# A mixture-of-experts stage on one Trainium2 core: the second layer's bias moved from a matmul into the copy out of PSUM

## The chip, the cores and the metric

The kernel runs on one core of one Trainium2 chip. The metric is the device time of one execution, in microseconds (us), lower is better. All inputs and outputs are float32 arrays in the chip's memory (HBM).

## The reference, cut to what matters

The program is one network of two layers on an input of 2 x 256 x 48 x 48. Layer 0 is a selective scan on images, layer 1 is attention and then a feed-forward block with eight experts, of which each of the 4608 tokens uses two. Only the last block is touched:

```python
logits = xf @ gate_w + gate_b
probs = softmax(logits)
top2_vals, top2_idx = top_k(probs, 2)
cw = zeros((N, 8)).at[arange(N)[:, None], top2_idx].add(top2_vals)
# for each expert, with bb1 of 512 and bb2 of 256 numbers:
h = gelu(xf @ w1 + bb1)
y = h @ w2 + bb2
acc = acc + we[:, None] * y
```

xf is 4608 x 256, w1 is 256 x 512, w2 is 512 x 256 for each expert.

## The kernel before, in words

The program is a row of phases with a barrier of all engines between them. The scan takes most of the span, then come the attention, a blend with the gate's logits, `gate_phase` (L1727) and `expert_phase` (L1956). The instructions of every engine are written out by hand in their order, with a semaphore for each hand-over. The experts' loop is unrolled.

`gate_phase` sorts the 9216 pairs of token and expert by expert and cuts the sorted list into 79 tiles (`TILES`) of 128 rows, each with one expert. It leaves `we["from"]` and `we["to"]` (the row numbers for gather and scatter), `we["own"]` (the expert of each tile, integers) and `we["sel"]`. It also splits the second layer's weights into a high part on ScalarE (L1829) and a low part on GpSimd (L1800), and makes `we["rows"]`: 40 partitions that hold the biases of the eight experts in rows 0 to 7 (high part) and 32 to 39 (low part, L1940), zero between; 512 columns of the first bias and 256 of the second.

`expert_phase` runs over the 79 tiles. For tile i:

- GpSimd gathers 128 rows of the tokens (`gather`, L1989) two tiles ahead, makes `sel` (L1994), a 40 x 128 matrix that has a one in the rows of the tile's expert, and scatters the tile's result (`scatter`, L1998).
- TensorE turns the rows (`turn_x`, L2032, two transposes), multiplies by the first layer (`up`): the bias comes first, as a matmul of `sel` with 512 columns of `rows` (L2040, 40 rows deep), then six matmuls of 512 columns (L2045 to L2047). It turns the hidden values (`turn_h`, L2055, four transposes) and multiplies by the second layer (`down`): the bias first, as a matmul of `sel` with 256 columns of `rows` (L2062, 40 rows deep), then twelve matmuls of 256 columns (L2067 to L2069). All products go as three passes of high and low parts.
- The weights are addressed with a register that `value_load` reads from `we["own"]` once per tile (before `up`).
- ScalarE makes the high part of x (L2100), the gelu (L2107) and the high part of h (L2113). VectorE makes the low parts (L2131, L2147) and copies the result out of PSUM into one of three buffers (`move_y`, L2137), which the scatter reads.

The order on TensorE is `up(i)`, `turn_x(i+1)`, `down(i-1)`, `turn_h(i)`, and on VectorE the low part of x(i+1), `move_y(i-1)`, the low part of h(i). In both, tile i-1's end lies between pieces of tile i:

```python
for i in range(TILES):
    e = pe.value_load(we["own"][0:1, i:i + 1], min_val=0, max_val=E - 1)
    up(i, e)
    if i + 1 < TILES:
        turn_x(i + 1)
    if i:
        down(i - 1, before)
    turn_h(i)
    before = e
```

After the loop SyncE waits for all scatters and loads the results back in 12 steps (L2023), VectorE joins them with their weights (L2157, L2163), TensorE turns them (L2091), ScalarE copies them (L2122) and stores. The loads go to three pairs of buffers: `yb00`, `yb01`, `yb10`, the memory of `table`, and that of `xy`.

Of the kernel before, what the change touches and what calls it, by code (L numbers as in the profile page):

```python
# [8 lines left out]
F32R = mybir.dt.float32r  # L9
U32 = mybir.dt.uint32  # L10
I32 = mybir.dt.int32
ALU = mybir.AluOpType
# [3 lines left out]
B, C, H, W = 2, 256, 48, 48  # L16
# [20 lines left out]
TT = 384  # L37
# [5 lines left out]
E, HF = 8, 512  # L43
HB = HF // 128
TILES = 2 * NT // 128 + E - 1
FAR = 8192
BROWS = 40
# [1679 lines left out]
def gate_phase(nc, P, w, keep, we, route):  # L1727
# [5 lines left out]
    with ExitStack() as ctx:  # L1733
        s = Space(nc, ctx, "gate")
        raw = [s.sb(f"raw{i}", [128, 2 * HF]) for i in range(2)]
        rows = s.sb("rows", [BROWS, HF + C])
        small = lambda name, n=E, dt=F32: s.sb(name, [128, KB, n], dt)
        dif = route["lg"]
        dif2, ex2, pick = (small(n, 2) for n in ("dif2", "ex2", "pick"))
# [11 lines left out]
        own = s.sb("own", [128, TILES])  # L1751
# [10 lines left out]
        hi_cut, lo_cut, rows_here, zeroed, rows_cut, zero_out = (s.sem(n) for n in ("hi_cut", "lo_cut", "rows_here", "zeroed", "rows_cut", "zero_out"))  # L1762
# [7 lines left out]
        @block.sync  # L1770
        def _(sp):
            def weights(n):
                if n >= 2:
                    sp.wait_ge(lo_cut, n - 1)
                sp.dma_start(raw[n % 2][:, :].rearrange("p (h n) -> p h n", h=HB), w["W2"][n].rearrange("(h p) n -> p h n", h=HB)).then_inc(raw_here[n % 2], 16)

            weights(0)
            weights(1)
            sp.wait_ge(zeroed, 1)
            sp.dma_start(P["xt"][0:1, :], rows[E:E + 1, 0:C]).then_inc(zero_out, 16)  # L1780
            for at in (0, 32):
                sp.dma_start(rows[at:at + E, 0:HF], w["b1"]).then_inc(rows_here, 16)
                sp.dma_start(rows[at:at + E, HF:HF + C], w["b2"]).then_inc(rows_here, 16)
            for n in range(2, E):
                weights(n)
            sp.wait_ge(zero_out, 16)
# [38 lines left out]
        @block.scalar  # L1825
        def _(act):
            def cut(n):
                act.wait_ge(raw_here[n % 2], 16 * (n // 2 + 1))
                act.activation(piece(n, "_hi"), raw[n % 2][:, :], ACT.Copy).then_inc(hi_cut, 1)  # L1829

            def name_low(b):
                act.wait_ge(e_done, b + 1)
                if b >= 2:
                    act.wait_ge(listed, b - 1)
                act.activation(hot_q[b % 2][:, :, 1, :], hot_e[b % 2][:, :, :], ACT.Identity, scale=row1[:, 0:1]).then_inc(l_done, 1)

            cut(0)
            cut(1)
            cut(2)
            act.wait_ge(step_done, 2)  # L1840
            act.activation(dif[:, :, :], dif[:, :, :], ACT.Exp).then_inc(ex_done, 1)
            act.activation(ex2[:, :, :], dif2[:, :, :], ACT.Exp).then_inc(ex_done, 1)
            cut(3)
            act.wait_ge(rows_here, 64)
            act.activation(we["rows"][:, :], rows[:, :], ACT.Copy).then_inc(rows_cut, 1)
            for n in range(4, E):
                cut(n)
            act.wait_ge(row_done, 2)
            for b in range(NH):
                name_low(b)  # L1850
# [102 lines left out]
            dve.tensor_tensor(we["to"][:, :], ids[:, :], spare[:, :], ALU.add)  # L1953


def expert_phase(nc, P, keep, acc, we, table, out):  # L1956


    with ExitStack() as ctx:
        s = Space(nc, ctx, "moe")  # L1960
        ring = lambda name, n, shape, dt=F32: [s.sb(f"{name}{i}", shape, dt) for i in range(n)]
        XR, YR = 3, 3
        xy = s.sb("xy", [128, XR + YR, C])
        xg, yo = [xy[:, i, :] for i in range(XR)], [xy[:, XR + i, :] for i in range(YR)]
        x_hi, x_lo = ring("x_hi", 2, [128, 2, 128], F32R), ring("x_lo", 2, [128, 2, 128], F32R)
        sel = ring("sel", 3, [BROWS, 128], F32R)
        g = ring("g", 2, [128, HF])
        h_hi, h_lo = ring("h_hi", 2, [128, HB, 128], F32R), ring("h_lo", 2, [128, HB, 128], F32R)
        TR = 3
        yb = [[s.sb(f"yb{i}{c}", [128, TT // 128, C])[:, :, :] for c in range(2 - i)] for i in range(TR - 1)] + [[xy[:, c * 3:c * 3 + 3, :] for c in range(2)]]  # L1970
        yb[1].append(table[:, 0:2 * TT].rearrange("p (a c) -> p a c", c=C))
        ps_x, ps_h, ps_t, ps_y = ([s.ps(f"{n}{i}", [128, 512]) for i in range(2)] for n in ("ps_x", "ps_h", "ps_t", "ps_y"))
        came = [s.sem(f"came{i}") for i in range(XR)]
        sent = [s.sem(f"sent{i}") for i in range(YR)]
        x_turned, xh_done, xl_done, up_done, g_done, h_turned, hh_done, hl_done, down_done, y_moved, sel_done = (
            s.sem(n) for n in ("x_turned", "xh_done", "xl_done", "up_done", "g_done", "h_turned", "hh_done", "hl_done", "down_done", "y_moved", "sel_done"))
        out_gone = s.sem("out_gone")
        y_here = [s.sem(f"y_here{i}") for i in range(TR)]
        first_done, both_done, back_done, out_done = (s.sem(n) for n in ("first_done", "both_done", "back_done", "out_done"))
        BL = TT // 128  # L1980
# [31 lines left out]

        @block.sync
        def _(sp):
            for k in range(YR):
                sp.wait_ge(sent[k], 16 * ((TILES + YR - 1 - k) // YR))

            for t in range(NTT):
                if t >= TR:
                    sp.wait_ge(back_done, t - TR + 1)  # L2020
                for c in range(2):
                    at = 1 + FAR * c + t * TT
                    sp.dma_start(yb[t % TR][c], P["y2"][at:at + TT, :].rearrange("(a p) n -> p a n", p=128)).then_inc(y_here[t % TR], 16)  # L2023

        @block.tensor
        def _(pe):
# [31 lines left out]
            def down(i, e):  # L2058
                if i >= 2:
                    pe.wait_ge(y_moved, i - 1)  # L2060
                o = ps_y[i % 2][:, 0:C]
                pe.matmul(o, sel[i % 3][:, :], we["rows"][:, HF:HF + C], start=True, stop=False)  # L2062
                pe.wait_ge(hl_done, i + 1)
                for b in range(HB):
                    w_hi = we["w2_hi"][:, bass.ds(e * (HB * C) + b * C, C)]
                    w_lo = we["w2_lo"][:, bass.ds(e * (HB * C) + b * C, C)]
                    pe.matmul(o, h_hi[i % 2][:, b, :], w_lo, start=False, stop=False)  # L2067
                    pe.matmul(o, h_lo[i % 2][:, b, :], w_hi, start=False, stop=False)  # L2068
                    mm = pe.matmul(o, h_hi[i % 2][:, b, :], w_hi, start=False, stop=b == HB - 1)  # L2069
                mm.then_inc(down_done, 1)  # L2070
# [3 lines left out]
            for i in range(TILES):  # L2074
                e = pe.value_load(we["own"][0:1, i:i + 1], min_val=0, max_val=E - 1)
# [50 lines left out]
        @block.vector  # L2126
        def _(dve):
            def cut_x(i):
                dve.wait_ge(xh_done, i + 1)
                v = lambda x: x[:, :, :].rearrange("p a b -> p (a b)")  # L2130
                dve.tensor_tensor(v(x_lo[i % 2]), ps_x[i % 2][:, 0:C], v(x_hi[i % 2]).bitcast(F32), ALU.subtract).then_inc(xl_done, 1)  # L2131

            def move_y(i):
                dve.wait_ge(down_done, i + 1)
                if i >= YR:
                    dve.wait_ge(sent[i % YR], 16 * (i // YR))
                dve.tensor_copy(yo[i % YR][:, :], ps_y[i % 2][:, 0:C]).then_inc(y_moved, 1)  # L2137

            cut_x(0)
            for i in range(TILES):  # L2140
                if i + 1 < TILES:
                    cut_x(i + 1)
                if i:
                    move_y(i - 1)
                dve.wait_ge(hh_done, i + 1)
                v = lambda x: x[:, :, :].rearrange("p a b -> p (a b)")
                dve.tensor_tensor(v(h_lo[i % 2]), ps_t[i % 2][:, :], v(h_hi[i % 2]).bitcast(F32), ALU.subtract).then_inc(hl_done, 1)  # L2147
            move_y(TILES - 1)

            half = lambda v: v.rearrange("p (h c) -> p h c", h=2)  # L2150

            def join(t):
                dve.wait_ge(y_here[t % TR], 32 * (t // TR + 1))
                for a in range(BL):
                    n = t * BL + a
                    v = half(yb[t % TR][0][:, a, :])
                    dve.scalar_tensor_tensor(v, v, we["v"][:, n, 0:1],  # L2157
                                             acc[:, :, n * 128:n * 128 + 128], ALU.mult, ALU.add).then_inc(first_done, 1)
                for a in range(BL):
                    n = t * BL + a  # L2160
                    dve.wait_ge(first_done, n + 1)
                    v = yb[t % TR][0][:, a, :]
                    dve.scalar_tensor_tensor(v, yb[t % TR][1][:, a, :], we["v"][:, n, 1:2], v, ALU.mult, ALU.add).then_inc(both_done, 1)  # L2163

            for t in range(NTT):
                join(t)


def conv_attn_hybrid_kernel(nc, x, w0, w1, out):
# [12 lines left out]
    with ExitStack() as ctx:  # L2182
# [41 lines left out]
        blend_phase(nc, P, w1, keep, t_hi, t_lo, o_t, den, we["w1_hi"], we["w1_lo"], route)  # L2224
        turns.close()
        we |= {n: s.sb(n, [128, E * HB * C], F32R) for n in ("w2_hi", "w2_lo")}
        we["rows"], we["sel"] = s.sb("rows", [BROWS, HF + C], F32R), s.sb("sel", [BROWS, TILES])
        we["v"], we["own"] = s.sb("v", [128, KB, 2]), s.sb("own", [1, TILES], I32)
        we["from"], we["to"] = s.sb("from", [128, TILES], I32), s.sb("to", [128, TILES], I32)
        gate_phase(nc, P, w1, keep, we, route)  # L2230
        expert_phase(nc, P, keep, o_t, we, table, out)


_L0 = ["ln_g", "ln_b", "skip_scale", "proj_W", "proj_b", "in_W", "conv_W", "conv_b", "x_proj_W", "dt_W", "dt_b",
# [19 lines left out]
```

## Time and profile before

| | |
|---|---|
| median of 3 runs | 5875.48 us (5871.67 to 5880.47) |
| the profiled execution's own time | 5875.91 us |
| its span in the trace | 5874.2 us |
| TensorE busy | 5065.8 us, 86% |
| GpSimd busy | 4271.6 us, 73% |
| VectorE busy | 4213.8 us, 72% |
| ScalarE busy | 3787.4 us, 64% |

PE is TensorE's matmuls, PEld its weight loads, DVE VectorE, ACT ScalarE, POOL GpSimd, SP SyncE. A matmul is shown from its start to a modelled end, and overlaps the next one, so the start-to-start distance is what it occupies. "[idle before <-x]" at a row's end says how long the engine had been idle and what ended that; "issue" means that it waited for nothing that the profile shows. The expert loop lies in the stretch from 5449 to 5822 us of the span, the loads and stores after it end the span.

### The profile page before, as it was taken

How to read it: one execution, taken by the hardware profiler on the slowest of the kernel's cores; microseconds unless marked ns; L12 is line 12 of the kernel's file. 1: busy time of each engine (PE TensorE's matmuls, PEld its weight loads, DVE VectorE, ACT ScalarE, POOL GpSimd, SP SyncE). 2: the span in 40 equal slices, each digit the busy share in tenths (PEclk: the TensorE clock that was granted, in tenths of full speed). 3: DMA queues.
4: the chain of work that ended last, by engine and by line, in shares of the span. 5: the costliest groups of instructions: out<-in, count | busy, mean ns of one | idle time of the engine just before them, and what ended most of it. 6: DMA issues, size and time to landing. Idle time of an engine off the chain costs nothing. (4 is left out here: it accounts for less than half of the span.)

```text
span 5874.2 us, 82875 instructions
## 1 busy us (share of the span) xinstructions
PE 5065.8 (86%) x21540; PEld 3376.1 (57%) x21540; DVE 4213.8 (72%) x4029; ACT 3787.4 (64%) x8376; POOL 4271.6 (73%) x2720
## 2 busy tenths in 40 slices
PE   4777388998899899889998999897799999995997
PEld 2344255555555555555555555554458888884675
DVE  3677599999999999999999999997751111118334
ACT  2566588888888888888888888885442222226332
POOL 0567699999999899999998999997504444444442
PEclk8888599999999999999999999998999999996998
DMA  3666677777777777777777777777500000004113
GB/s 94 171 198 205 209 235 247 249 246 251 240 246 248 241 247 246 244 248 243 243 249 239 248 245 247 249 248 263 194 23 1 0 0 0 0 0 123 50 58 132
DMA packets 395504, 1045.37 MB, mean 178 GB/s; under 512 B 53422, under 2 KB 90319, under 8 KB 390944
## 3 DMA queue, kind: packets, MB, share of 16 engines
q1 hardware_dynamic: 382464, 1010.05, 54.1%
q0 software_dynamic: 7584, 20.72, 1.1%
q10 hardware_dynamic: 4992, 9.44, 0.4%
q8 instruction: 166, 2.72, 0.2%
q14 instruction: 298, 2.44, 0.1%
HBM read 869.23 MB, written 170.79 MB: 177 GB/s over the span
## 5 line engine op out<-in xcount | busy, mean ns | idle before, releaser
L920 POOL TENSOR_TENSOR scan_hc<-scan_h,scan_c_rep 128x768 f32<-128x768 f32 x1536 | 2749.2, 1821 | 233.9 <-PE scan_ps_y L751 177.2
L751 PE MATMUL scan_ps_y<-scan_hc,keep_ident 128*128 128x512 f32 (+1 forms) x6144 | 2219.8, 489 | 23.4 <-ACT scan_y L786 23.0
L885 DVE TENSOR_TENSOR_SCAN scan_h<-scan_da,scan_h,scan_ps_p 128x768 f32<-128x768 f32 x896 | 1568.7, 1796 | 0.0
L751 PEld LDWEIGHTS scan_ps_y<-scan_hc,keep_ident 128*128 128x128 f32 x6144 | 1067.9, 190 | 824.1 <-issue 739.3
L803 ACT ACTIVATE scan_warm<-scan_du_t 128x128 f32<-128x128 f32 x4608 | 1423.6, 388 | 38.7 <-PE scan_ps_p L742 32.9
L842 ACT ACTIVATE scan_da<-scan_dd,layer_a_neg 128x768 f32<-128x768 f32 x1344 | 1184.8, 922 | 4.4 <-issue 3.6
L1464 POOL TENSOR_TENSOR attn_e_lo<-attn_e,attn_e_hi 128x512 fp32r<-128x512 f32 x324 | 418.1, 1290 | 610.9 <-DVE attn_e_hi L1455 610.9
L742 PE MATMUL scan_ps_p<-keep_ident,scan_warm 128*128 128x128 f32 x4608 | 647.9, 277 | 222.2 <-DVE scan_h L885 221.3
L885 DVE TENSOR_TENSOR_SCAN scan_h<-scan_da,scan_ps_p 128x768 f32<-128x768 f32 x448 | 758.9, 1735 | 2.3 <-ACT scan_da L842 2.0
L742 PEld LDWEIGHTS scan_ps_p<-keep_ident,scan_warm 128*128 128x128 f32 x4608 | 532.7, 141 | 372.2 <-issue 156.9
L864 DVE TENSOR_TENSOR scan_ps_p<-scan_ps_p,scan_dd 128x768 f32<-128x768 f32 x576 | 547.5, 951 | 194.2 <-PE scan_ps_p L734 193.0
L1455 DVE CAST attn_e_hi<-attn_e 128x512 fp32r<-128x512 f32 x324 | 145.8, 450 | 725.4 <-ACT attn_e L1443 725.4
L1443 ACT ACTIVATE attn_e<-attn_ps_s 128x512 f32<-128x512 f32 x324 | 193.8, 598 | 708.1 <-PE attn_ps_s L74 708.1
L734 PE MATMUL scan_ps_p<-scan_cut,layer_b_sel 128*128 128x512 f32 (+1 forms) x1152 | 381.8, 413 | 57.4 <-DVE scan_h L885 47.8
L842 ACT ACTIVATE scan_ps_p<-scan_dd,layer_a_neg 128x768 f32<-128x768 f32 x192 | 172.2, 897 | 274.9 <-DVE scan_h L885 274.9
L914 POOL TENSOR_TENSOR scan_bu<-scan_dd,scan_b_rep 128x768 f32<-128x768 f32 x192 | 348.2, 1814 | 0.0
L575 POOL TENSOR_TENSOR delta_de<-delta_de,delta_du 128x768 f32<-128x768 f32 x96 | 173.1, 1811 | 193.5 <-ACT delta_du L488 193.5
L734 PEld LDWEIGHTS scan_ps_p<-scan_cut,layer_b_sel 128*128 128x128 f32 x1152 | 196.4, 190 | 156.0 <-DVE scan_h L885 131.8
L74 PE MATMUL attn_ps_o<-attn_e_hi,t_hi 128*128 128x512 f32 x648 | 257.9, 398 | 0.0
L74 PE MATMUL attn_ps_s<-f_hi 128*128 x648 | 257.1, 397 | 0.0
L73 PE MATMUL attn_ps_o<-attn_e_lo,t_hi 128*128 128x512 f32 x648 | 256.8, 396 | 0.0
L72 PE MATMUL attn_ps_o<-attn_e_hi,t_lo 128*128 128x512 f32 x648 | 256.3, 396 | 0.0
(328 smaller groups left out, 6910.4 us busy)
## 6 DMA issues: line engine op xcount, KB each, us to landing
scan_c_rep<-bc_dram SPq DMA_DIRECT2D x1536, 384.0 KB, 4.2
scan_dd<-dd_dram SPq DMA_DIRECT2D x96, 768.0 KB, 5.7
scan_b_rep<-bc_dram SPq DMA_DIRECT2D x192, 384.0 KB, 4.9
dd_dram<-delta_de SPq DMA_DIRECT2D x96, 384.0 KB, 2.6
dd_dram<-delta_du SPq DMA_DIRECT2D x96, 384.0 KB, 3.2
y_dram<-scan_y SPq DMA_DIRECT2D x96, 384.0 KB, 4.6
mid_nat<-y_dram SPq DMA_DIRECT2D x48, 384.0 KB, 7.8
delta_img<-xn_dram SPq DMA_DIRECT2D x16, 576.0 KB, 8.6
```

What stands on the lines that cost most here:

```text
L73: pe.matmul(out, wh, xl, start=False, stop=False)
L74: return pe.matmul(out, wh, xh, start=False, stop=stop)
L734: mm = pe.matmul(ps_p[place(t) % PR][:, lo:hi], keep["b_sel"][:, n, :], cut[st % 2][:, lo:hi], start=True, stop=True)
L742: mm = pe.transpose(ps_p[place(t) % PR][:, b * 128:b * 128 + 128], warm[w % WR][:, b, :], keep["ident"][:, :])
L751: mm = pe.matmul(ps_y[:, lo:hi], keep["ident"][:, :], hc[t % HR][:, lo:hi], start=n == 0, stop=n == N - 1)
L803: last = act.activation(warm[w % WR][:, b, :], du_t[st % 2][:, b * 128:b * 128 + 128], ACT.Identity, scale=du_t[st % 2][:, at:at + 1])
L842: act.activation(dst, dd[st % 2][:, 0, :], ACT.Exp, scale=keep["a_neg"][:, k, n:n + 1]).then_inc(ex_done, 1)
L864: dve.tensor_tensor(x, x, dd[st % 2][:, 1, :], ALU.mult).then_inc(mult_done, 1)
L885: dve.tensor_tensor_scan(view(h[n]), view(x), view(y), start, ALU.mult, ALU.add).then_inc(scan_done, 1)
L914: pool.tensor_tensor(bu[f % SR][:, :], dd[st % 2][:, 1, :], b_rep[f % SR][:, :], ALU.mult).then_inc(bu_done, 1)
L920: pool.tensor_tensor(hc[t % HR][:, :], h[t % N][:, :], c_rep[t % CR][:, :], ALU.mult).then_inc(hc_done, 1)
L1464: pool.tensor_tensor(e_lo[j % 3][:, :], e[j % 3][:, :], e_hi[j % 3][:, :].bitcast(F32), ALU.subtract).then_inc(lo_done, 1)
```

## The change

The 40-row table keeps the first layer's bias alone (512 columns in place of 768), and the matmul L2062 is gone. The first of the twelve matmuls of `down` now opens the accumulation. At the start of the phase SyncE issues one DMA that copies the second layer's 8 x 256 biases to every one of the 128 partitions (2048 numbers each, 1 MB written), into a new tile `desk`, which after the loop serves as three of the buffers that the results are loaded back to. VectorE waits for it once, ahead of the loop. In `move_y` VectorE now loads the tile's expert number into a register of its own and adds, in place of copying, PSUM and the 256 columns of `desk` that the register names. In `gate_phase` the two small DMAs of the second bias go, and the copy and the low part of `rows` are 512 columns wide.

```diff
-        rows = s.sb("rows", [BROWS, HF + C])
+        rows = s.sb("rows", [BROWS, HF])
...
                 sp.dma_start(rows[at:at + E, 0:HF], w["b1"]).then_inc(rows_here, 16)
-                sp.dma_start(rows[at:at + E, HF:HF + C], w["b2"]).then_inc(rows_here, 16)
...
-            act.wait_ge(rows_here, 64)
+            act.wait_ge(rows_here, 32)
...
-        yb = [[s.sb(f"yb{i}{c}", [128, TT // 128, C])[:, :, :] for c in range(2 - i)] for i in range(TR - 1)] + [[xy[:, c * 3:c * 3 + 3, :] for c in range(2)]]
-        yb[1].append(table[:, 0:2 * TT].rearrange("p (a c) -> p a c", c=C))
+        desk = s.sb("desk", [128, 3, 2 * TT])
+        add_y = desk[:, :, :].rearrange("p a c -> p (a c)")[:, 0:E * C]
+        third = lambda x: x.rearrange("p (a c) -> p a c", c=C)
+        yb = [[third(desk[:, 0, :]), third(desk[:, 1, :])], [third(desk[:, 2, :]), third(table[:, 0:2 * TT])], [xy[:, c * 3:c * 3 + 3, :] for c in range(2)]]
...
         @block.sync
         def _(sp):
+            sp.dma_start(add_y, w["b2"].rearrange("e c -> (e c)").partition_broadcast(128)).then_inc(add_here, 16)
...
                 o = ps_y[i % 2][:, 0:C]
-                pe.matmul(o, sel[i % 3][:, :], we["rows"][:, HF:HF + C], start=True, stop=False)
                 pe.wait_ge(hl_done, i + 1)
...
-                    pe.matmul(o, h_hi[i % 2][:, b, :], w_lo, start=False, stop=False)
+                    pe.matmul(o, h_hi[i % 2][:, b, :], w_lo, start=b == 0, stop=False)
...
-                dve.tensor_copy(yo[i % YR][:, :], ps_y[i % 2][:, 0:C]).then_inc(y_moved, 1)
+                e = dve.value_load(we["own"][0:1, i:i + 1], min_val=0, max_val=E - 1)
+                dve.tensor_tensor(yo[i % YR][:, :], ps_y[i % 2][:, 0:C], add_y[:, bass.ds(e * C, C)], ALU.add).then_inc(y_moved, 1)
 
             cut_x(0)
+            dve.wait_ge(add_here, 16)
```

On TensorE, between `turn_x` and the twelve matmuls of `down`, there stood before:

```order
L2047 MATMUL moe_ps_h<-w_hi,moe_x_hi 128x512
L2032 MATMUL moe_ps_x<-keep_ident,moe_xy 128x128 x2
L2062 MATMUL moe_ps_y<-keep_rows,moe_sel 128x256
L2067 REGISTER_ALU
L2067 MATMUL moe_ps_y<-keep_w_lo,moe_h_hi 128x256
L2068 REGISTER_ALU
L2068 MATMUL moe_ps_y<-keep_w_hi,moe_h_lo 128x256
L2069 MATMUL moe_ps_y<-keep_w_hi,moe_h_hi 128x256
```

and now (the lines of `down` are one further, those of `turn_x` and `up` two):

```order
L2049 MATMUL moe_ps_h<-w_hi,moe_x_hi 128x512
L2034 MATMUL moe_ps_x<-keep_ident,moe_xy 128x128 x2
L2068 REGISTER_ALU
L2068 MATMUL moe_ps_y<-keep_w_lo,moe_h_hi 128x256
L2069 REGISTER_ALU
L2069 MATMUL moe_ps_y<-keep_w_hi,moe_h_lo 128x256
L2070 MATMUL moe_ps_y<-keep_w_hi,moe_h_hi 128x256
```

One matmul per tile is gone, 79 in all, and a matmul of full depth follows the transposes directly; nothing else of TensorE's order moved.

On VectorE one tile of the loop read before (`xh_done`, `down_done` and `hh_done` are the semaphores of x's high part, of `down` and of h's high part):

```order
L2131 TENSOR_TENSOR moe_x_lo<-moe_ps_x,moe_x_hi 128x256 [waits moe_xh_done]
L2137 COPY moe_xy<-moe_ps_y 128x256 [waits moe_down_done]
L2147 TENSOR_TENSOR moe_h_lo<-moe_ps_t,moe_h_hi 128x512 [waits moe_hh_done]
L2131 TENSOR_TENSOR moe_x_lo<-moe_ps_x,moe_x_hi 128x256 [waits moe_xh_done]
L2137 COPY moe_xy<-moe_ps_y 128x256 [waits moe_down_done]
```

and now:

```order
L2132 TENSOR_TENSOR moe_x_lo<-moe_ps_x,moe_x_hi 128x256 [waits moe_xh_done]
L2138 TENSOR_LOAD keep_own [waits moe_down_done]
L2138 ISA x2
L2139 ISA
L2139 TENSOR_TENSOR moe_xy<-moe_ps_y,moe_desk 128x256
L2150 TENSOR_TENSOR moe_h_lo<-moe_ps_t,moe_h_hi 128x512 [waits moe_hh_done]
```

The register load and three register instructions stand behind the wait for `down`, ahead of the addition, and the low part of h is behind all of them.

## Rows read from the trace of the kernel before

**Rows 1.** Busy time of each engine in two stretches; clock, DMA share, GB/s at the end
```profile
5455.00:5820.00 365.00, 363.56 (x2040) 282.50 (x2038) 120.94 (x235) 116.00 (x237) 172.58 (x231) 0.99 0.17 56
5820.00:5875.00 55.00, 20.13 (x84) 15.12 (x84) 29.82 (x73) 10.47 (x24) 0.97 (x1) 0.54 0.78 262
```

**Rows 2.** Timeline, TensorE around L2062 in one tile: start us, us, instruction
```profile
5603.90 0.38 PE L2032 MATMUL moe_ps_x<-keep_ident,moe_xy 128*128 128x128 f32 x2
...
5604.21 0.18 PEld L2062 LDWEIGHTS moe_ps_y<-keep_rows,moe_sel 40*128 40x128 f32 x1 [0.17 <-issue]
5604.21 0.38 PE L2062 MATMUL moe_ps_y<-keep_rows,moe_sel 40*128 40x256 f32 x1
5604.52 0.19 PEld L2067 LDWEIGHTS moe_ps_y<-keep_w_lo,moe_h_hi 128*128 128x128 f32 x1
5604.52 0.39 PE L2067 MATMUL moe_ps_y<-keep_w_lo,moe_h_hi 128*128 x1
...
5604.62 0.19 PEld L2068 LDWEIGHTS moe_ps_y<-keep_w_hi,moe_h_lo 128*128 128x128 f32 x1
5604.74 0.28 PE L2068 MATMUL moe_ps_y<-keep_w_hi,moe_h_lo 128*128 x1
...
5604.86 0.29 PE L2069 MATMUL moe_ps_y<-keep_w_hi,moe_h_hi 128*128 x1
...
5605.95 0.47 PEld L2055 LDWEIGHTS moe_ps_t<-keep_ident,moe_g 128*128 128x128 f32 x4
5606.05 0.60 PE L2055 MATMUL moe_ps_t<-keep_ident,moe_g 128*128 128x128 f32 x4
...
5608.81 0.38 PE L2062 MATMUL moe_ps_y<-keep_rows,moe_sel 40*128 40x256 f32 x1
```

**Rows 3.** Timeline of TensorE in the scan: 16-row transposes followed by 128-row matmuls
```profile
3977.71 0.54 PE L725 MATMUL scan_ps_p<-keep_ident,scan_rows 16*128 16x16 f32 x6
3978.30 0.62 PE L734 MATMUL scan_ps_p<-scan_cut,layer_b_sel 128*128 128x512 f32 x2
...
3978.30 0.30 PEld L734 LDWEIGHTS scan_ps_p<-scan_cut,layer_b_sel 128*128 128x128 f32 x2
```

**Rows 4.** Timeline of TensorE in the scan: 128-row transposes followed by 128-row matmuls
```profile
3001.78 0.84 PE L742 MATMUL scan_ps_p<-keep_ident,scan_warm 128*128 128x128 f32 x6
3002.46 1.02 PE L751 MATMUL scan_ps_y<-scan_hc,keep_ident 128*128 128x512 f32 x2
...
3002.35 0.30 PEld L751 LDWEIGHTS scan_ps_y<-scan_hc,keep_ident 128*128 128x128 f32 x2
```

**Rows 5.** Timeline, VectorE in the same tile as rows 2
```profile
5606.25 0.42 DVE L2137 COPY moe_xy<-moe_ps_y 128x256 f32<-128x256 f32 x1 [0.82 <-PE moe_ps_y L2069]
...
5607.32 0.69 DVE L2147 TENSOR_TENSOR moe_h_lo<-moe_ps_t,moe_h_hi 128x512 fp32r<-128x512 f32 x1 [0.64 <-ACT moe_h_hi L2113]
```

**Rows 6.** Timeline, end of the gate phase and the first tiles
```profile
5446.39 0.95 DVE L1940 TENSOR_TENSOR keep_rows<-gate_rows,keep_rows 8x768 fp32r<-8x768 f32 x1
...
5449.72 1.17 POOL L1989 DMA_INDIRECT moe_xy<-xt_dram,keep_from  x1 [24.27 <-POOLq L1733]
...
5452.76 0.69 PE L2032 MATMUL moe_ps_x<-keep_ident,moe_xy 128*128 128x128 f32 x2 [6.37 <-DMA moe_xy<-xt_dram,keep_from]
...
5453.65 0.78 PE L2040 MATMUL moe_ps_h<-keep_rows,moe_sel 40*128 40x512 f32 x1 [0.21 <-issue]
...
5458.34 0.42 DVE L2131 TENSOR_TENSOR moe_x_lo<-moe_ps_x,moe_x_hi 128x256 fp32r<-128x256 f32 x1 [4.01 <-ACT moe_x_hi L2100]
```

**Rows 7.** Timeline, the last tile
```profile
5818.08 0.42 DVE L2137 COPY moe_xy<-moe_ps_y 128x256 f32<-128x256 f32 x1 [2.63 <-PE moe_ps_y L2069]
...
5818.41 0.38 PE L2062 MATMUL moe_ps_y<-keep_rows,moe_sel 40*128 40x256 f32 x1
...
5819.15 0.69 DVE L2147 TENSOR_TENSOR moe_h_lo<-moe_ps_t,moe_h_hi 128x512 fp32r<-128x512 f32 x1 [0.64 <-ACT moe_h_hi L2113]
...
5819.97 0.36 PE L2067 MATMUL moe_ps_y<-keep_w_lo,moe_h_hi 128*128 x1 [1.18 <-DVE moe_h_lo L2147]
```

More of the change, by code:

```diff
@@ L1953, in _, with expert_phase @@
             dve.tensor_tensor(we["to"][:, :], ids[:, :], spare[:, :], ALU.add)
-def expert_phase(nc, P, keep, acc, we, table, out):
+def expert_phase(nc, P, w, keep, acc, we, table, out):
     with ExitStack() as ctx:
@@ L1976, in expert_phase @@
             s.sem(n) for n in ("x_turned", "xh_done", "xl_done", "up_done", "g_done", "h_turned", "hh_done", "hl_done", "down_done", "y_moved", "sel_done"))
-        out_gone = s.sem("out_gone")
+        out_gone, add_here = s.sem("out_gone"), s.sem("add_here")
         y_here = [s.sem(f"y_here{i}") for i in range(TR)]
@@ L2226, in conv_attn_hybrid_kernel @@
         we |= {n: s.sb(n, [128, E * HB * C], F32R) for n in ("w2_hi", "w2_lo")}
-        we["rows"], we["sel"] = s.sb("rows", [BROWS, HF + C], F32R), s.sb("sel", [BROWS, TILES])
+        we["rows"], we["sel"] = s.sb("rows", [BROWS, HF], F32R), s.sb("sel", [BROWS, TILES])
         we["v"], we["own"] = s.sb("v", [128, KB, 2]), s.sb("own", [1, TILES], I32)
@@ L2230, in conv_attn_hybrid_kernel @@
         gate_phase(nc, P, w1, keep, we, route)
-        expert_phase(nc, P, keep, o_t, we, table, out)
+        expert_phase(nc, P, w1, keep, o_t, we, table, out)
 _L0 = ["ln_g", "ln_b", "skip_scale", "proj_W", "proj_b", "in_W", "conv_W", "conv_b", "x_proj_W", "dt_W", "dt_b",
```

## The prediction

> **What bounds the kernel now.** Read first the busy time by stretch, over the experts' loop [rows 1]: of 365 us TensorE is busy for 363.56, VectorE for 120.94, ScalarE for 116.00, GpSimd for 172.58, at full clock (0.99). The loop is TensorE's, and the other engines only matter by when they answer. Then the timeline of one tile [rows 2]: the bias matmul L2062 starts at 5604.21 and again at 5608.81, so a tile takes 4.60 us, and 79 tiles make the loop. The reader is to look in rows 2 at where each weight load (PEld) starts against its matmul (PE). For L2068 the load starts 0.12 us ahead of its matmul, beside the matmul before; the same for L2055. For L2062 and for L2067, the one right behind it, load and matmul start together: the load lies open. Third, VectorE's rows of that tile [rows 5], for how late its work may come, and last the two ends of the loop [rows 6, 7], for the new DMA and for what the tail waits on.
>
> **The matmul that goes.** From the start of the two transposes L2032 (5603.90) to the start of L2068 (5604.74) there are 0.84 us [rows 2]. Without L2062, and with every load hidden, the same stretch is two transposes and one matmul of 256 columns. A 128-row transpose takes 0.11 us start to start (six in 0.84 with the last one's 0.28: (0.84 - 0.28) / 5) [rows 4], a 256-column matmul 0.12 (5604.74 to 5604.86) [rows 2]: 0.34 us. So up to 0.84 - 0.34 = **0.50 us a tile** go. Of this, 0.31 are L2062's own distance to L2067 (5604.21 to 5604.52), the rest is what the switch to 40 rows and back adds to its two neighbours: L2067 occupies 0.22 in place of 0.12, and L2062 starts 0.20 in place of 0.11 after the second transpose.
>
> Does the rest go too? It depends on why L2067's load isn't hidden. Two readings: the change of depth from 40 rows to 128, or the wait and register instruction ahead of L2067, which stay. The wait is a poor cause: L2055 also stands behind waits, and its load is hidden (5605.95 against 5606.05) [rows 2]; L2068 stands behind a register instruction and is hidden too. The depth is the better one: in the scan a 128-row matmul follows 16-row transposes, and its load starts with it, at 3978.30, after the last of these has ended (3977.71 + 0.54) [rows 3]; where 128-row matmuls follow 128-row transposes the load starts at 3002.35, 0.11 ahead of its matmul and while the transposes still run [rows 4]. The changed kernel has the latter case: L2034 (128 rows), then L2068 (128 rows). I take 0.50 us. The lower bound is 0.31.
>
> Here two rules of the Trainium skill part. "TensorE: Matmul & The Clock Gate", in Part 3 on packing small matmuls, says that a weight load overlaps matmuls in flight only when its row group differs; by it a full-depth load behind full-depth transposes would stay open, and the sum would have 0.31 a tile. "TensorEngine Tiling (Array Packing)", Key Properties, says that changing the tiling mode drains the engine; by it the sum has 0.50. The trace agrees with the second and not with the first (rows 4, a load at 3002.35 beside transposes of the same depth).
>
> How often: all tiles but the last. In the last one L2062 starts at 5818.41 and L2067 at 5819.97, released by the low part of h [rows 7]: the bias matmul lies in a gap. 78 x 0.50 = **-39.0 us** (lower bound 78 x 0.31 = -24.2).
>
> **The addition in place of the copy.** The two read the same 256 columns of PSUM and write the same buffer; the nearest row for the addition is L2131 at 0.42 us [rows 6], a tensor_tensor of PSUM and SBUF of that size, and the copy takes 0.42 [rows 5]. Nothing.
>
> **The register load on VectorE.** No row shows a TENSOR_LOAD. On TensorE one stands, with two ISA instructions, between the first two transposes and the first L2040: 5452.76 to 5453.65 = 0.89 us, of which the transposes take most [rows 6]. So for the load and its companions, L, the rows give between 0 and 0.89; VectorE has three companions, not two, and can't start before `down` has ended. I take 0.8, near the upper row. Is it hidden? After the copy (ends 5606.67) VectorE waits until 5607.32, so 0.65 are free; the low part of h then ends at 5608.01, and the down matmuls that want it start at 5608.81 (0.80 later, 0.7 with the new order) [rows 2, 5]. So L up to about 1.3 costs nothing in the loop. As a cycle: from L2067's start to the copy's 1.73 us (5604.52 to 5606.25), less the 0.10 that L2067 loses, then L, 0.42 of addition, 0.69 of low part, some 0.05 of hand-overs: 2.79 + L against a tile of 4.10. The cover is the `up` of the next tile; without it L would be paid in full. It is paid at the end: the last `move_y` is alone (+0.8), and the one before it, at 5818.08, now ends at 5819.30, so that the last low part of h starts 0.2 later than 5819.15 [rows 7]. **+1.0 us**. The skill has a price for the load: "DMA: Bandwidth & Descriptors", Latency and other measured facts, gives a tensor_load a floor of about 600 ns; no run here shows it, and with 0.6 in place of 0.8 the sum would be 0.3 lower.
>
> **The scatter behind it.** GpSimd's scatter waits for `y_moved` and stands ahead of the next gather, so both move by L. GpSimd is busy 172.58 of 365 us [rows 1], and a gather is issued two tiles, over 8 us, ahead of its transposes. Nothing.
>
> **The broadcast.** SyncE writes 1.05 MB (128 x 8 KB) while the first gather is under way: the gather starts at 5449.72 and the first transposes wait for it until 5452.76, idle 6.37 us [rows 6]. At the 262 GB/s of the tail [rows 1] the broadcast takes 4.0 us. Bounds: the gather is served beside it as if alone, 0; or wholly behind it, 4.0. I take the middle, **+2.0 us**. The wait on VectorE costs nothing: it stands ahead of the x part of tile 1, at 5458.34, over 8 us after the phase's start [rows 6].
>
> **The gate phase.** The low part of `rows` (0.95 us for 768 columns) is in VectorE's chain that ends the phase [rows 6]; with 512 columns it takes 0.95 x 512/768 = 0.63: **-0.3 us**. The missing small DMAs, the narrower copy and fill lie on engines that are waiting there. Nothing.
>
> **The tail.** Same number and size of loads, to other addresses; `desk` is read last long before the loads, which wait for all scatters. Nothing.
>
> **Sum**: -39.0 + 1.0 + 2.0 - 0.3 = -36.3. The profiled execution took 5875.9, hence 5839.6; the median of the runs is 0.4 below it, hence **5839 us**.
>
> **The rivals.**
> - *The open load stays* (0.31 a tile). For it: in the trace no 128-row matmul of this reduced type behind transposes is looked at in this loop, and the wait for h's low part stays ahead of it. Against it: rows 3 and 4. -24.2 + 2.7 = -21.5: 5854 us. The first of the skill's two rules above gives the same.
> - *VectorE's chain binds in part*: L between 1.3 and 1.8. At 1.6 a tile is 4.39 and 78 x 0.21 = 16.4 are gained: about 5862 us. Against it: 0.89 is more than TensorE's load can have taken.
> - *Slower: VectorE's chain becomes the bound.* The register load begins only when `down(i-1)` has ended, the low part of h(i) stands behind it, and `down(i)` waits for that. At L = 2.0 a tile takes 4.79 us in place of 4.60: 78 x 0.19 = +14.8, with +2 for the gather and +3 at the end about 5895 us. It decides from L = 1.81. For it: nothing measures the load on VectorE. Against it: the same 0.89.
> - *No difference*: L near 1.8, or a bound in the loop that these rows don't show (a late gather, instruction supply) that holds the tile at 4.6 us. 5875 us. That the change doesn't do what it says can be set aside: the order has the 79 matmuls gone.
>
> **How the numbers follow.** Forecast 0.64; load stays open 0.22; VectorE in part 0.06; slower 0.05; no difference 0.03. About 0.2% (12 us) is what a measurement of this kernel can tell from no change; the three runs lie within 9 us. Faster by more: 0.64 + 0.22 + 0.06 = 0.92; same 0.03; slower 0.05. The forecast's own range is 5875.5 - 39.0 - 0.3, with 0 to 4.0 for the gather and 0 to 1.8 for the end: 5836 to 5842, and some 3 us more on either side for the runs' scatter. The rival at 0.31 gives with the same bounds up to 5857. Range 5833 to 5858.
>
> **What would show it.** The distance from one tile to the next 4.10 us, TensorE still busy throughout; the weight load of the first `down` matmul 0.1 us ahead of its matmul (if it starts with it, the first rival holds, with 4.3 us a tile). VectorE: the addition at 0.42 us, its idle time before it longer by L, the low part of h still released by ScalarE or by VectorE's own row before it, never TensorE waiting for it except in the last tile. The first transposes at 5452.8 + 0 to 4 us. The tail unchanged in length. The prediction is wrong in its reason if TensorE's idle time names VectorE's low part of h in every tile.

## The result, and the profile after

| | before | changed |
|---|---|---|
| median | 5875.46 us (5863.97 to 5880.47, 5 runs) | 5829.36 us (5825.08 to 5840.02, 5 runs) |
| span of the profiled execution | 5874.2 us | 5827.6 us |
| TensorE busy | 5065.8 us | 5022.8 us |

The ratio is 0.9934, with a 95% interval of 0.9922 to 0.9945: 32 to 46 us less. The forecast was 5839 us, 36 less. Cut at four points of the two traces, the spans differ like this:

| stretch | before | changed | difference |
|---|---|---|---|
| start to the first gather's issue | 5449.72 | 5440.25 | -9.47 |
| to the first transposes | 3.04 | 4.34 | +1.30 |
| to the start of the last `move_y` operation | 368.90 | 329.69 | -39.21 |
| to the end | 52.54 | 53.32 | +0.78 |

Only the middle two rows are the change's. The first is nearly all run-to-run spread of phases that the change leaves alone: over the twelve profiled executions of this study the first gather was issued between 5438.78 and 5454.61 us, whichever kernel it was, and the changed kernel and its variants spread over that whole width. The change's own part of it is the narrower low part of `rows`, 0.27 us (below).

The changed kernel's busy time by stretch, as [rows 1] (PE, PEld, DVE, ACT, POOL, then clock, DMA share, GB/s), over the loop and over what follows it:

```profile
5450.00:5774.00 324.00, 321.92 (x1964) 264.40 (x1964) 113.93 (x235) 115.19 (x235) 172.20 (x229) 1.00 0.19 63
5774.00:5827.00 53.00, 18.49 (x72) 13.69 (x72) 29.90 (x73) 10.46 (x24) 0.97 (x1) 0.53 0.80 270
```

TensorE is still busy throughout. The timeline of the changed kernel around the place where L2062 stood, as [rows 2]:

```profile
5604.20 0.38 PE L2034 MATMUL moe_ps_x<-keep_ident,moe_xy 128*128 128x128 f32 x2
5604.31 0.19 PEld L2068 LDWEIGHTS moe_ps_y<-keep_w_lo,moe_h_hi 128*128 128x128 f32 x1
5604.33 0.36 PE L2068 MATMUL moe_ps_y<-keep_w_lo,moe_h_hi 128*128 x1
...
5604.41 0.19 PEld L2069 LDWEIGHTS moe_ps_y<-keep_w_hi,moe_h_lo 128*128 128x128 f32 x1
5604.53 0.28 PE L2069 MATMUL moe_ps_y<-keep_w_hi,moe_h_lo 128*128 x1
...
5605.72 0.28 PE L2070 MATMUL moe_ps_y<-keep_w_hi,moe_h_hi 128*128 x1
...
5608.43 0.36 PE L2068 MATMUL moe_ps_y<-keep_w_lo,moe_h_hi 128*128 x1
```

From 5604.33 to 5608.43 there are 4.10 us, as forecast. From the first transposes to L2069 there are 0.33 us (0.84 before). The load is hidden: L2069 follows its two predecessors without the 0.1 or 0.2 us that each neighbour lost before. How it is split between them differs a little from the forecast: L2068's load is shown only 0.02 us ahead of its matmul, and L2068 occupies 0.20 us, but it already starts 0.13 after the pair of transposes does.

VectorE in the same tile, as [rows 5]:

```profile
5606.76 0.42 DVE L2139 TENSOR_TENSOR moe_xy<-moe_ps_y,moe_desk 128x256 f32<-128x256 f32 x1 [1.03 <-issue]
...
5607.10 0.69 DVE L2150 TENSOR_TENSOR moe_h_lo<-moe_ps_t,moe_h_hi 128x512 fp32r<-128x512 f32 x1
```

The addition takes the copy's 0.42 us. It starts 1.04 us after the last `down` matmul does (5605.72), where the copy started 0.32 after (5605.93 to 5606.25): the register load and what belongs to it take 0.72. The low part of h has no idle time before it now; it ends at 5607.79, and TensorE wants it at 5608.43, so 0.64 us are left. As many are left in the run without the load (below, 0.64): the 0.72 just fill the time in which VectorE waited for ScalarE before. What the 0.72 are made of stands in the view of one source line, L2138, with the smallest, median and largest duration in ns:

```profile
L2138 DVEq TENSOR_LOAD <-keep_own x79: 299/304/559, 5454.3 to 5773.6; - x79
L2138 DVEq FUSED_REGOPS  x79: 190/190/210, 5454.9 to 5773.9; - x79
L2138 DVEq SEQ_ASSERT  x79: 23/23/41, 5455.2 to 5774.1; - x79
```

0.30 us of load, 0.19 and 0.02 of register work and check, 0.06 more at L2139, and 0.15 between them. The same view of the kernel before would have given the price on TensorE's queue:

```profile
L2075 PEldq TENSOR_LOAD <-keep_own x79: 297/302/491, 5452.8 to 5812.2; - x79
L2075 PEldq FUSED_REGOPS  x79: 151/151/165, 5453.3 to 5812.6; - x79
L2075 PEldq SEQ_ASSERT  x79: 18/18/32, 5453.6 to 5812.8; - x79
```

The end of the gate phase and the start of the loop, as [rows 6], with SyncE's issue of the broadcast:

```profile
5437.18 0.68 DVE L1939 TENSOR_TENSOR keep_rows<-gate_rows,keep_rows 8x512 fp32r<-8x512 f32 x1
...
5439.48 0.36 SPq L2016 DMA_DIRECT2D moe_desk<-in_L_ffn_b  x1
...
5440.25 1.17 POOL L1990 DMA_INDIRECT moe_xy<-xt_dram,keep_from  x1 [24.01 <-POOLq L1733]
...
5444.59 0.69 PE L2034 MATMUL moe_ps_x<-keep_ident,moe_xy 128*128 128x128 f32 x2 [7.41 <-DMA moe_xy<-xt_dram,keep_from]
...
5450.24 0.42 DVE L2132 TENSOR_TENSOR moe_x_lo<-moe_ps_x,moe_x_hi 128x256 fp32r<-128x256 f32 x1 [4.09 <-ACT moe_x_hi L2101]
```

The broadcast is issued 0.8 us before the first gather, and the gather's rows are there 4.34 us after its issue in place of 3.04. L2132, which waits for the broadcast too, is released by ScalarE.

### The profile page after: what moved, and what is told of

The parts are those of the page before. It is cut to its first block and busy times, and to the rows that moved or that the text cites. A ratio compares the mean times of both kernels' runs of the same rounds, so it can differ in the third digit from the quotient of the medians.

```text
span 5827.6 us, 83110 instructions
## 1 busy us (share of the span) xinstructions
PE 5022.8 (86%) x21461; PEld 3357.0 (58%) x21461; DVE 4205.6 (72%) x4029; ACT 3787.0 (65%) x8376; POOL 4271.0 (73%) x2720
```

## The experiments

Four questions were open: whether the 0.19 us beyond the bias matmul's own 0.31 come from its depth; whether VectorE's part is free; how far the register load may grow; and whether the broadcast is what delays the first gather. For each kernel three numbers are read from the trace: the time of a tile (median distance of the `turn_x` transposes), the loop (first transposes to the start of the last copy or addition, 368.90 before and 329.69 changed), and the start (first gather's issue to the first transposes, 3.04 and 4.34). They don't carry the spread of the phases ahead. The ratios are taken against runs of the kernel before that were made beside each group of runs: their median was 5868.48 us beside the kernels with 96 rows and with two loads; of the others, 5873.81 beside those up to "Both bias matmuls at full depth" and 5865.88 beside those after it. So whole times of different groups don't compare to better than some 10 us.

### The matmul alone

```diff
-                pe.matmul(o, sel[i % 3][:, :], we["rows"][:, HF:HF + C], start=True, stop=False)
...
-                    pe.matmul(o, h_hi[i % 2][:, b, :], w_lo, start=False, stop=False)
+                    pe.matmul(o, h_hi[i % 2][:, b, :], w_lo, start=b == 0, stop=False)
```

> The kernel before without the second layer's bias matmul and with the plain copy kept; the second bias is left out of the result. Theory (the matmul's 0.31 us and the 0.19 us by which the change between 40 and 128 rows of depth holds up its neighbours both go, and nothing on VectorE matters): a tile takes 4.10 us as in the changed kernel, the weight load of the first down matmul starts 0.1 us ahead of it, the stretch from the first transposes to the last copy is 39 us shorter than before (368.9 to about 330), the first gather lands 3.0 us after its issue as before, since there is no broadcast. Rival (VectorE's addition or the register load has a part in the gain, or costs some of it inside the loop): a tile takes something other than 4.10 us.

Measured: 5827.19 us (5822.33 to 5836.72), ratio 0.9918 (0.9902 to 0.9935). A tile 4.10 us, loop 328.96, start 2.93. Two successive rows of its timeline:

```profile
5601.03 0.38 PE L2032 MATMUL moe_ps_x<-keep_ident,moe_xy 128*128 128x128 f32 x2
...
5605.14 0.38 PE L2032 MATMUL moe_ps_x<-keep_ident,moe_xy 128*128 128x128 f32 x2
```

The matmul is the whole gain, 39.94 us of the loop. The changed kernel's loop is 0.73 longer: one register load, the last one, which nothing hides. The delay at the start is absent without the broadcast.

### The bias matmul kept, at full depth

```diff
-BROWS = 40
+BROWS = 128
...
-                pe.matmul(o, sel[i % 3][:, :], we["rows"][:, 0:HF], start=True, stop=False)
+                pe.matmul(o, sel[i % 3][0:40, :], we["rows"][0:40, 0:HF], start=True, stop=False)
```

> The kernel before, all its work kept, but the 40-row table and sel are 128 rows (the new rows are zero) and the second layer's bias matmul uses all 128; the first layer's still uses 40. Theory (the change of depth leaves the loads open): the load of the bias matmul and of the one behind it are hidden, the bias matmul then occupies only its 256 columns, 0.12 us, and a tile takes 4.10 + 0.12 = 4.22 us in place of 4.60; stretch 368.9 - 78 x 0.38 = 339. Rival (the wait, the register instruction or the start of an accumulation leaves the load open, not the depth): nothing changes, 4.60 us a tile; or if a deeper matmul costs more, longer.

Measured: 5838.04 us (5826.79 to 5842.5), ratio 0.9933 (0.9914 to 0.9952). A tile 4.21 us, loop 338.02. Its timeline at the bias matmul:

```profile
5600.81 0.38 PE L2032 MATMUL moe_ps_x<-keep_ident,moe_xy 128*128 128x128 f32 x2
5600.92 0.19 PEld L2062 LDWEIGHTS moe_ps_y<-keep_rows,moe_sel 128*128 128x128 f32 x1
5600.94 0.36 PE L2062 MATMUL moe_ps_y<-keep_rows,moe_sel 128*128 128x256 f32 x1
...
5601.02 0.19 PEld L2067 LDWEIGHTS moe_ps_y<-keep_w_lo,moe_h_hi 128*128 128x128 f32 x1
5601.15 0.28 PE L2067 MATMUL moe_ps_y<-keep_w_lo,moe_h_hi 128*128 x1
```

L2067's load starts 0.13 us ahead of its matmul, though the wait and the register instruction ahead of it are still there and L2067 doesn't open the accumulation. So the depth is the cause (on TensorE nothing else was changed), and of the 0.51 us that the change took from a tile only 0.11 are the matmul's work; 0.40 are the switch to 40 rows and back. More than three quarters of the gain were to be had with the matmul in place.

### Sixty-four and ninety-six rows

```diff
-BROWS = 40
+BROWS = 64
```

> The kernel before with both bias matmuls 64 rows deep in place of 40, the new rows zero. Theory (what counts is a depth different from the neighbours' 128): 4.60 us a tile, no change. Rival (what counts is that 40 is no multiple of 32 or 64): the loads are hidden, and a tile takes 3.84 us.

Measured: 5868.74 us (one run). A tile 4.61 us, loop 368.90, to the hundredth that of the kernel before.

```profile
5602.27 0.38 PE L2062 MATMUL moe_ps_y<-keep_rows,moe_sel 64*128 64x256 f32 x1
...
5606.89 0.38 PE L2062 MATMUL moe_ps_y<-keep_rows,moe_sel 64*128 64x256 f32 x1
```

With `BROWS = 96`:

> The kernel before with both bias matmuls 96 rows deep, the new rows zero. Theory (a matmul holds up its neighbours when the chip runs it at another depth than theirs, and 96 rows count as 128): 3.83 us a tile as with 128. Rival (any depth but 128 is another one): 4.60 us a tile as with 40 and 64.

Measured: 5810.39 us (one run). A tile 3.83 us, loop 307.73.

```profile
5603.23 0.38 PE L2032 MATMUL moe_ps_x<-keep_ident,moe_xy 128*128 128x128 f32 x2
5603.37 0.36 PE L2062 MATMUL moe_ps_y<-keep_rows,moe_sel 96*128 96x256 f32 x1
```

96 rows go like 128, 64 go like 40. That fits the Trainium skill's "TensorEngine Tiling (Array Packing)", Available Configurations and Key Properties, which knows modes of 64 and of 32 rows beside the full one and says that changing the mode drains the engine. The page doesn't say which mode a matmul of 40 or 96 rows gets, and no run here lies between 64 and 96.

### Both bias matmuls at full depth

```diff
-BROWS = 40
+BROWS = 128
```

> The kernel before with both bias matmuls 128 rows deep, the new rows zero. Theory: beside the 0.38 us at the second layer's bias, 0.38 us go at the first layer's (its own 0.43 to 0.235, the one behind it 0.33 to 0.235, its start 0.20 to 0.11 after the transposes): 3.84 us a tile, stretch 368.9 - 79 x 0.76 = 309, so about 5816 us and faster than the changed kernel, although no matmul is taken out. Rival (loads open for another reason): 4.60 us a tile. A second rival: another engine's chain binds before 3.84 (GpSimd's gather and scatter are 2.9 us a tile, VectorE's chain 2.8): a tile between 3.84 and 4.2.

Measured: 5808.22 us (5806.61 to 5810.88), ratio 0.9888 (0.9871 to 0.9904). A tile 3.83 us, loop 307.73.

```profile
5599.85 0.60 PE L2055 MATMUL moe_ps_t<-keep_ident,moe_g 128*128 128x128 f32 x4
...
5600.17 0.19 PEld L2040 LDWEIGHTS moe_ps_h<-keep_rows,moe_sel 128*128 128x128 f32 x1
5600.20 0.48 PE L2040 MATMUL moe_ps_h<-keep_rows,moe_sel 128*128 128x512 f32 x1
...
5600.52 0.39 PE L2045 MATMUL moe_ps_h<-w_lo,moe_x_hi 128*128 x1
...
5604.03 0.48 PE L2040 MATMUL moe_ps_h<-keep_rows,moe_sel 128*128 128x512 f32 x1
```

One constant gives 61 us of loop, against 39 of the change: the first layer's bias matmul loses another 0.38 us a tile in the same way. No other engine binds at 3.83.

### The change with the first bias at full depth

The changed kernel with `BROWS = 128`.

> The changed kernel with the first layer's bias matmul 128 rows deep (40-row table and sel grown to 128 rows, the new ones zero). Theory (depth): another 0.38 us a tile go, 4.10 - 0.39 = 3.71 us a tile; stretch from first transposes to last addition 329.7 - 79 x 0.39 = 299; some 30 us under the changed kernel. Rival (VectorE's chain, 2.79 us plus the 0.72 us that the register load took in the changed kernel's trace = 3.51, or GpSimd's own sum binds): more than 3.71 us a tile, and TensorE's idle time names VectorE.

Measured: 5815.65 us (5808.83 to 5827.49), ratio 0.9919 (0.9901 to 0.9938). A tile 3.80 us, not 3.71; loop 307.42, not 299. The rival holds in that TensorE now waits for VectorE, though the forecast 3.51 us of VectorE's chain would not have done it. VectorE's rows of two tiles, the first `down` matmuls, and ScalarE's high part of h in the second tile:

```profile
5702.21 0.43 DVE L2139 TENSOR_TENSOR moe_xy<-moe_ps_y,moe_desk 128x256 f32<-128x256 f32 x1 [1.14 <-issue]
5702.60 0.69 DVE L2150 TENSOR_TENSOR moe_h_lo<-moe_ps_t,moe_h_hi 128x512 fp32r<-128x512 f32 x1
...
5703.53 0.35 PE L2068 MATMUL moe_ps_y<-keep_w_lo,moe_h_hi 128*128 x1
...
5705.03 0.60 PE L2057 MATMUL moe_ps_t<-keep_ident,moe_g 128*128 128x128 f32 x4
...
5705.79 0.60 ACT L2114 ACTIVATE moe_h_hi<-moe_ps_t 128x512 fp32r<-128x512 f32 x1 [1.38 <-PE moe_ps_t L2057]
...
5705.95 0.42 DVE L2139 TENSOR_TENSOR moe_xy<-moe_ps_y,moe_desk 128x256 f32<-128x256 f32 x1 [1.09 <-issue]
...
5706.42 0.69 DVE L2150 TENSOR_TENSOR moe_h_lo<-moe_ps_t,moe_h_hi 128x512 fp32r<-128x512 f32 x1
...
5707.35 0.36 PE L2068 MATMUL moe_ps_y<-keep_w_lo,moe_h_hi 128*128 x1
```

L2068 starts 0.93 us after the low part of h does, both times, that is 0.24 after it ends, and so it is (0.23 to 0.25) in 76 of 76 tiles looked at: VectorE releases it. What the low part waits for is another matter. Where a tile is bound by the addition alone, the low part starts 0.07 to 0.09 us before the addition's drawn end, as with three loads (5706.16 + 0.43 and 5706.51). That holds for 23 tiles here: three long ones (4.01 to 5.07 us), and 20 of 3.69 to 3.72 us, in which ScalarE's high part of h (L2114) also ends 0.03 us ahead, so that the two are level. In the other 53 the low part starts later than that against the addition, and 0.03 us after the high part ends, as at 5706.42 (5705.79 + 0.60 = 5706.39); these tiles take 3.81 in the mean. In them the high part starts up to 0.85 us after the first of the transposes L2057 (0.76 at 5705.79), where it starts after 0.64 in the 20 level tiles and in the changed kernel. What holds it back there stays open.

In the loop the change buys nothing here: with both depths mended, the kernel with the bias matmul (loop 307.73) and the one without it (307.42) are equal, and the latter pays 1.7 us more at the start (4.71 against 3.03), for the broadcast. What the page calls idle hides this: TensorE's row for that wait has only 1.3 us in two waits, since a matmul is drawn longer than it occupies the engine. The expectation that the idle time would name VectorE was wrong; the start-to-start distances show it.

### No register load, two, and three

Without it, with expert 0's columns for all tiles:

```diff
-                e = dve.value_load(we["own"][0:1, i:i + 1], min_val=0, max_val=E - 1)
-                dve.tensor_tensor(yo[i % YR][:, :], ps_y[i % 2][:, 0:C], add_y[:, bass.ds(e * C, C)], ALU.add).then_inc(y_moved, 1)
+                dve.tensor_tensor(yo[i % YR][:, :], ps_y[i % 2][:, 0:C], add_y[:, 0:C], ALU.add).then_inc(y_moved, 1)
```

> The changed kernel without the register load: the addition always takes expert 0's 256 columns, so the second bias is wrong for the other experts. Theory (the load is hidden in the loop and is paid at the end alone): 4.10 us a tile as with it; from the start of the last down matmul to the start of the addition 0.32 us in place of 1.04; the low part of h waits for ScalarE again, not for the addition; the span is 1 us shorter. Rival (the load costs something in the loop): a tile under 4.10 us.

Measured: 5827.17 us (one run). A tile 4.10 us, loop 328.84, that is 0.85 less than the changed kernel's.

```profile
5703.13 0.42 DVE L2138 TENSOR_TENSOR moe_xy<-moe_ps_y,moe_desk 128x256 f32<-128x256 f32 x1 [0.31 <-PE moe_ps_y L2070]
...
5704.19 0.69 DVE L2149 TENSOR_TENSOR moe_h_lo<-moe_ps_t,moe_h_hi 128x512 fp32r<-128x512 f32 x1 [0.64 <-ACT moe_h_hi L2114]
```

With the load's line repeated, three times:

> The changed kernel with the register load made three times ahead of the addition. Theory (VectorE's chain takes 2.79 us + L a tile, and binds once that is over 4.10, that is from L = 1.3; slower than before from L = 1.8): three loads make L = 0.72 + 2 x 0.6 to 0.7 = 1.9 to 2.1, a tile 4.7 to 4.9 us, the whole 5875 + 78 x (0.1 to 0.3) + 3 = 5886 to 5901, slower than the kernel before; TensorE waits in every tile for the low part of h. Rival (loads pipeline, or the chain has more room than the rows say): under 4.60 us a tile.

Measured: 5908.74 us (5887.48 to 5911.56), ratio 1.006 (1.0041 to 1.008): slower than the kernel before. A tile 4.92 us, loop 400.67.

```profile
5704.00 0.60 PE L2057 MATMUL moe_ps_t<-keep_ident,moe_g 128*128 128x128 f32 x4
...
5706.16 0.43 DVE L2141 TENSOR_TENSOR moe_xy<-moe_ps_y,moe_desk 128x256 f32<-128x256 f32 x1 [3.11 <-issue]
...
5706.51 0.68 DVE L2152 TENSOR_TENSOR moe_h_lo<-moe_ps_t,moe_h_hi 128x512 fp32r<-128x512 f32 x1
...
5707.42 0.36 PE L2068 MATMUL moe_ps_y<-keep_w_lo,moe_h_hi 128*128 x1 [0.58 <-DVE moe_h_lo L2152]
```

From the last `down` matmul (5703.88) to the addition 2.28 us: three loads take 2.28 - 0.32 = 1.96. TensorE now waits for VectorE's low part of h. The mechanism is the expected one, but the sizes lie above it: a tile of 4.92 against 4.7 to 4.9, and 5908.74 us against 5886 to 5901. And twice:

> The changed kernel with the register load made twice ahead of the addition. From the runs with one load (L = 0.72) and with three (L = 1.96, 4.92 us a tile) VectorE's chain is 2.96 + L once it binds. Theory (one chain, so linear): L = 1.34, a tile 4.30 us, TensorE waits for the low part of h in every tile; the whole 78 x 0.20 = 16 us above the changed kernel, still some 30 us below the kernel before. Rival (my first working, 2.79 + L): 4.13 us a tile and nothing to be seen in the time.

Measured: 5853.04 us (5848.28 to 5865.7), ratio 0.9969 (0.9957 to 0.998). A tile 4.30 us.

```profile
5705.90 0.42 DVE L2140 TENSOR_TENSOR moe_xy<-moe_ps_y,moe_desk 128x256 f32<-128x256 f32 x1 [1.85 <-issue]
5706.25 0.68 DVE L2151 TENSOR_TENSOR moe_h_lo<-moe_ps_t,moe_h_hi 128x512 fp32r<-128x512 f32 x1
...
5707.16 0.36 PE L2068 MATMUL moe_ps_y<-keep_w_lo,moe_h_hi 128*128 x1
```

The median tile is as expected, but the loop is 351.66, 22.0 us above the changed kernel's in place of 16: some tiles take 4.44 to 4.68 us, and the second takes 5.38. In the longer ones the addition starts 1.8 to 2.0 us after the last `down` matmul in place of 1.65, so the two loads took longer there; why is open. So L is 0, 0.72, 1.33 and 1.96 for none to three loads, and a tile takes 4.10, 4.10, 4.30 and 4.92: flat, then a slope of one. The slope begins at L = 4.10 - 2.96 = 1.14; the kernel before is met at 4.61 - 2.96 = 1.65.

### The register load ahead of the wait, and the broadcast after the first gather

```diff
-BROWS = 40
+BROWS = 128
...
+            sp.wait_ge(came[0], 16)
             sp.dma_start(add_y, w["b2"].rearrange("e c -> (e c)").partition_broadcast(128)).then_inc(add_here, 16)
...
             def move_y(i):
+                e = dve.value_load(we["own"][0:1, i:i + 1], min_val=0, max_val=E - 1)
                 dve.wait_ge(down_done, i + 1)
...
-                e = dve.value_load(we["own"][0:1, i:i + 1], min_val=0, max_val=E - 1)
```

> The changed kernel with the 128-row bias of the first layer, the register load ahead of the wait for down, and the broadcast issued only when the first gather has landed. Theory: 3.71 us a tile as with the depth alone (the load was hidden); the first transposes 3.0 us after the first gather's issue in place of 4.3; the addition 0.3 to 0.4 us after the last down matmul in place of 1.04; so about 2 to 3 us below the kernel with the depth alone, 46 + 30 + 2 = 78 us below the kernel before, about 5797. Rival (the broadcast now meets the gathers of the next tiles and holds up one that is needed): the first tiles longer, nothing gained at the start.

Measured: 5799.39 us (5795.06 to 5805.84), ratio 0.9882 (0.9866 to 0.9899), the fastest kernel here. A tile 3.72 us, loop 299.80, start 2.97.

```profile
5702.31 0.42 DVE L2140 TENSOR_TENSOR moe_xy<-moe_ps_y,moe_desk 128x256 f32<-128x256 f32 x1 [0.43 <-PE moe_ps_y L2071]
...
5703.27 0.69 DVE L2151 TENSOR_TENSOR moe_h_lo<-moe_ps_t,moe_h_hi 128x512 fp32r<-128x512 f32 x1 [0.53 <-ACT moe_h_hi L2115]
...
5704.21 0.37 PE L2069 MATMUL moe_ps_y<-keep_w_lo,moe_h_hi 128*128 x1
```

Both parts show in the stretch that each belongs to. With the load ahead of the wait the low part of h is released by ScalarE again and a tile is 3.72 us, so the load behind the wait is what cost the kernel with the depth alone its 7.6 us of loop (0.9 of them in one tile, 5.05 against 4.11 us); my expectation had it hidden. Held back until the first gather has landed, the broadcast costs nothing that the start shows: 2.97 us at the start, against 4.3 to 4.8 in the five kernels that issue it first. The low part of h ends at 5703.96, 0.25 us ahead of L2069: no more than the hand-over measured above, while L2069 also starts 0.14 after the first of the two transposes, as where nothing waits. So TensorE's own work and the chain over ScalarE and VectorE are level at 3.72, and by these rows less work on TensorE alone would gain little more (not tried). Expected were 78 us below the kernel before; the ratio gives 59 to 79. Against the kernel with both bias matmuls at full depth the loop is 7.9 us shorter; the intervals of the two ratios overlap, so the whole times don't separate them.

## Why the prediction was right, point by point

**The matmul that goes** was right in mechanism and size. 78 x 0.50 = 39.0 were forecast, 39.94 measured alone; a tile went from 4.61 to 4.10 us. The choice of 0.50 over 0.31, the depth and not the wait, was argued from the scan's rows [rows 3, 4] and is now shown: with the wait kept and the depth changed the load is hidden. Of the two rules of the Trainium skill, the trace agrees with the one on mode switching ("TensorEngine Tiling (Array Packing)", Key Properties) in that a change of depth costs time, 0.40 us here. It doesn't agree with the one in "TensorE: Matmul & The Clock Gate", Part 3, that a load overlaps only matmuls of another row group: the full-depth load of L2067 starts at 5601.02, 0.13 us ahead of its matmul, while the full-depth L2062 of 5600.94 runs. The forecast understated this cause: it counted 0.31 us as the matmul's own, but that too was mostly the open load; only 0.11 is.

**The addition in place of the copy**, forecast to cost nothing, was right: both take 0.42 us.

**The register load** was taken at 0.8 and measured 0.72. "No row shows a TENSOR_LOAD" is true of the rows shown and false of the trace. The timelines leave such instructions out; the view of the line L2075 has them at 0.30 us with 0.15 and 0.02 of register work, so the bounds of 0 to 0.89 were wider than they had to be. The end cost 0.73, not 1.0: the last low part of h was not delayed, since it starts at 5770.93, 0.03 us after ScalarE's high part ends (5770.30 + 0.60).

**The cycle** of 2.79 + L was the term that was mis-sized: measured 2.96 + L. Two pieces of it were too small. I took off 0.10 us for L2067's open load, but where TensorE waits the first `down` matmul still occupies 0.20 us in place of 0.12 (three loads, 5707.42 to 5707.62). And I took 0.05 for all hand-overs, where the one from the low part of h to the matmul is 0.24 alone; the low part starting 0.08 before the drawn end of the addition takes some of that back. In the forecast this cost nothing, because 0.72 lies below either threshold (1.14, not 1.3; the kernel before is met at 1.65, not 1.81). It doesn't explain the kernel with the first bias mended either: 2.96 + 0.72 = 3.68 is still under TensorE's own 3.72, and the tile of 3.80 comes mostly from the 53 tiles in which ScalarE's high part of h is late. The slack of 0.80 us after the low part of h was misread: it was counted to L2062, which doesn't need it, while L2067, which does, starts 1.1 us after it. The 0.7 taken for the new order was nearly right (0.64).

**The broadcast** was forecast at +2.0, the middle between bounds of 0 and 4.0, and measured +1.3 in the changed kernel and 1.3 to 1.8 over the five kernels that issue it first. It was right in kind, shown by the start at 2.93 without it and 2.97 with it held back; that the middle came so near is luck.

**The gate phase** was forecast at -0.3; the low part of `rows` went from 0.95 to 0.68 us.

**The tail** was taken as unchanged. It is 53.32 us against 52.54; over the twelve profiled executions it lies between 50.8 and 53.7, with no order by kernel, so the 0.8 is no effect that can be claimed.

**The sum** was -36.3, and the terms as measured give -39.9 + 0.7 + 1.3 - 0.3 = -38.2. The ratio's middle, 0.9934, makes 38.8 us of 5875. The medians' 46 is further off; in the profiled executions, whose times are within 0.5 us of the medians, the difference lies in the phases ahead, which ran 9.5 us shorter in the changed kernel's. Their spread from run to run is as large as that.

**The rivals**: the load of the first `down` matmul did not stay open. VectorE's chain bound neither in part nor wholly in the changed kernel, but both can be brought about: two loads give the first (4.30 us a tile), three the second (4.92), at 5908.74 us.

## What to carry to other kernels

A small matmul of fewer rows than its neighbours is dear not by its work but by what it does to them: look at where each weight load starts against its matmul, and before taking such a matmul out, pad it with zero rows to the neighbours' depth. Work moved off the bounding engine is free only while its new place has slack in its own chain, so a load or a register read that depends on nothing belongs ahead of the wait, not behind it. And look up sequencer instructions under their source line; a timeline that doesn't list them is no sign that the trace has no price for them.

## What the runs showed of the hardware that was not expected

- A 40-row matmul of 256 columns between 128-row ones costs 0.51 us where its work at full depth costs 0.11; one of 512 columns costs 0.38 us more than at 128 rows. 64 rows behave like 40 to the hundredth (4.61 us a tile), 96 like 128 (3.83).
- Reading one integer from SBUF into a VectorE register takes 0.30 us and with its register work 0.72 us ahead of the operation that uses it; each further one adds 0.62. The Trainium skill's "DMA: Bandwidth & Descriptors", Latency and other measured facts, has about 600 ns as the floor of a tensor_load. The trace doesn't agree: the instruction is 304 ns in the middle here, and only the whole group is above that figure.
- A matmul that waits for an operand starts 0.24 us after VectorE's operation on it ends, and the matmul after it starts 0.08 us later than usual (L2068 to L2069 is 0.20 us at 5707.42 with three loads, 0.12 between others).
